# The first expert slot interleaved with the drain of a fused decoder layer, and the order at the slots' ends

## What is computed

```
x = layernorm(x + retention(x))                 # decay mask, group norm over heads and time
x = layernorm(x + cross_attention(x, ctx))      # 16 heads of 16, causal softmax
x = layernorm(x + moe(x))                       # 8 experts, 2 of 8 per token

logits = xf @ router_w.T;  probs = softmax(logits);  topk_probs, topk_idx = top_k(probs, 2)
topk_probs = topk_probs / sum(topk_probs)
h   = gelu_tanh(xf @ w_fc[e] + b_fc[e])         # 256 -> 1024
out = h @ w_proj[e] + b_proj[e]                 # 1024 -> 256, weighted and summed over the 2 experts
```

## Time and profile before

| | |
|---|---|
| median of 3 runs | 1047.76 us (1046.54 to 1048.6) |
| the profiled execution | 1047.56 us, span 1045.7 us |
| TensorE busy | 966.0 us (92%), 11474 matmuls |
| VectorE, ScalarE, GpSimd busy | 640.7 (61%), 585.7 (56%), 371.9 us (36%) |
| sequences, from 0 to | 529 us |
| drain, then slot 0 | 529 to 559 us, 559 to 578 us |
| slots 1 to 35 | 578 to 1012 us |
| output norms | 1012 to 1046 us |

### The profile page before, as it was taken

One profiled execution on the slowest core, in us unless ns is written; L12 is line 12 of the kernel. 1 busy time (PEld: TensorE's weight loads), 2 busy tenths in 40 slices (PEclk: granted clock), 3 DMA queues, 4 the chain that ended last, 5 costly groups with the idle time before them and its releaser, 6 DMA issues.

```text
span 1045.7 us, 31053 instructions
## 1 busy us (share of the span) xinstructions
PE 966.0 (92%) x11474; PEld 875.3 (84%) x11474; DVE 640.7 (61%) x1952; ACT 585.7 (56%) x1531; POOL 371.9 (36%) x630
## 2 busy tenths in 40 slices
PE   6799999999999999999988998999999999999960
PEld 4688888888888888888866998999999999999960
DVE  2466767767667677777754575565564665564436
ACT  3355555555555565655544565565665675566534
POOL 0224444544445444444443422222322222223323
PEclk9899999999999999999979999999999999999985
DMA  7101151111111111111211425422525432522327
GB/s 265 55 22 53 42 175 55 40 62 42 53 62 37 58 43 52 48 47 55 85 42 37 78 41 132 128 44 42 140 42 136 103 73 42 133 48 41 50 35 317
DMA packets 56931, 79.93 MB, mean 76 GB/s; under 512 B 5680, under 2 KB 45872, under 8 KB 56560
## 3 DMA queue, kind: packets, MB, share of 16 engines
q1 hardware_dynamic: 41072, 58.50, 17.5%
q0 software_dynamic: 13536, 18.16, 10.3%
q10 hardware_dynamic: 2208, 1.73, 0.6%
HBM read 52.10 MB, written 29.71 MB: 78 GB/s over the span
## 4 chain that ended last, share of the span: by engine, by line
PE 67%; DVE 15%; issue 5%; ACT 5%; POOL 4%; DMA 3%; SPq 1%; ACTq 0%; DVEq 0%; POOLq 0%
PE bank L703 16%; PE bank L716 16%; DVE row_max L1045 7%; PE bank L468 5%; PE bank L583 3%; PE bank L483 3%; PE bank L458 3%; PE bank L536 3%; PE bank L628 3%; PE bank L508 3%; ACT h_f L967 2%; PE bank L614 2%; PE bank L503 2%; POOL grstd L1384 2%; DVE x_pre L1076 1%
## 5 line engine op out<-in xcount | busy, mean ns | idle before, releaser
L961 ACT ACTIVATE h_hi<-bank,bfc_s 128x256 fp32r<-128x256 f32 x288 | 139.6, 485 | 173.1 <-PE bank L703 171.0
L1247 DVE TENSOR_TENSOR h_lo<-h_f,h_hi 128x256 fp32r<-128x256 f32 x288 | 122.6, 426 | 175.6 <-ACT h_f L967 173.2
L1426 POOL DMA_INDIRECT residual_sum<-y_w,meta_i x72 | 116.6, 1620 | 319.0 <-DVE y_w L1271 299.1
L703 PE MATMUL bank<-xs_hi,w_hi 128*128 128x256 f32 x576 | 167.4, 291 | 8.1 <-DVE xs_lo L1217 7.8
L716 PE MATMUL bank<-w_hi,h_hi 128*128 128x256 f32 x576 | 163.5, 284 | 1.3 <-DVE h_lo L1247 1.3
L716 PE MATMUL bank<-w_hi,h_lo 128*128 128x256 f32 x576 | 163.3, 283 | 0.0
L703 PE MATMUL bank<-xs_lo,w_hi 128*128 128x256 f32 x576 | 163.2, 283 | 0.0
L703 PE MATMUL bank<-xs_hi,w_lo 128*128 128x256 f32 x576 | 162.8, 283 | 0.0
L716 PE MATMUL bank<-w_lo,h_hi 128*128 128x256 f32 x576 | 162.7, 282 | 0.0
L967 ACT ACTIVATE h_f<-bank,bfc_s 128x256 f32<-128x256 f32 x288 | 139.2, 483 | 0.7 <-DVE h_lo L1247 0.7
L703 PEld LDWEIGHTS bank<-xs_hi,w_hi 128*128 128x128 f32 x576 | 109.8, 191 | 9.7 <-issue 9.7
(11 more groups left out here) (167 smaller groups left out, 1977.3 us busy)
## 6 DMA issues: line engine op xcount, KB each, us to landing
rows<-sent_rows SPq DMA_DIRECT2D x37, 258.0 KB
...
```

The costliest lines, as they stand in the source:

```text
L703: last = mm(ps_h[j % 4][:, 0:SLOT], w[:, at:at + P], v[:, k, :], start=(n == 0), stop=(n == 3 * NCH - 1))
L961: A(h_hi[j % 4][:, :], ps_h[j % 4][:, 0:SLOT], ACT.Gelu_apprx_tanh, bias=bias)
L1247: V.tensor_tensor(h_lo[j % 4][:, :], h_f[j % 2][:, :], h_hi[j % 4][:, :].bitcast(f32), ALU.subtract).then_inc(s["h_split"], 1)
L1426: G.indirect_dma_start(total, bass.IndirectOffsetOnAxis(meta_i[:, half:half + 1], 0), y_w[:, half, :], None, compute_op=ALU.add)\
```

## The change

1. **Slot 0 inside the drain.** Its fc and proj stand one by one between the stages of sequences 29 to 31 (`fc0`, `proj0` on PE, `hidden` on ACT, `hidden_low` on DVE), and the 21 idle matmuls are gone. Its hidden columns lie in half of `ps_prep` instead of four banks, so fc j waits for the Gelus of fc j-1. The rows of slot 1 are turned into `ps_y`. `rank_out`, `copies_last`, `last_norms` stand beside slot 1 now, `rank_last`, `last_places` beside slot 2, `count_next` beside slot 3.
2. **The last norm ahead.** In step 31 the maxima of sequence 30 and what follows move from the step to the drain; `ln1_sum` and `ln1_norm` of sequence 31 stand before three of the four maxima, `x1_turn` and the turn of slot 0's rows before `max_turn`. On POOL `shares` of that step stands behind the norm's power.
3. **Low half of the next rows ahead of weights.** `split_rows(g + 1)` moves in front of `last_hi` and the last `split_lo` in a slot.
4. SPLIT is B - 12: the first expert's weights are split one step earlier. On POOL `add(0)` stands before the last sequence's second power, and `add(1)` before its `shares` and `send`.

```diff
-SPLIT = B - 11
+SPLIT = B - 12
...
-        ps_h = bank[0:4]
-        ps_xs = ps_prep
+        def ps_h(g, j):
+
+            if isinstance(g, int) and g == 0:
+                return ps_prep[:, 0:SLOT]
+            return bank[j % 4][:, 0:SLOT]
+
+        def ps_xs(g):
+
+            return ps_y if isinstance(g, int) and g == 1 else ps_prep
...
             def fc(g, j, whi, wlo):
 
-                if j >= 4:
+                if isinstance(g, int) and g == 0:
+                    if j >= 1:
+                        pe.wait_ge(s["h_done"], j + EVER)
+                elif j >= 4:
                     pe.wait_ge(s["h_done"], HC * g + j - 3 + EVER)
                 else:
                     pe.wait_ge(s["h_done"], HC * g + EVER)
+                if isinstance(g, int) and g == 1 and j < NT:
+                    pe.wait_ge(s["att_exp"], 4 * (B - 1) + j + 1)
...
             def rank_out(j):
 
-                if j == 0:
-                    logits(At(B - 2))
                 if j == 1:
                     o_turn(At(B - 1))
                 if j == 3:
                     att_back(At(B - 1))
                 if j == 4:
                     att_proj(At(B - 1))
+                if j == 6:
                     rank(At(B - 2))
                 if j == 8:
                     x2_turn(At(B - 1))
@@ -752,42 +773,55 @@
 
             def drain():
 
-                idle(DRAIN_IDLE)
+                x1_turn(At(B - 1))
+                pe.wait_ge(s["v_out"], B)
+                pe.sem_inc(s["rows_turned"], EVER)
+                turn_rows(0)
+                max_turn(At(B - 2))
+                o_turn(At(B - 3))
+                qx(At(B - 1))
                 att_back(At(B - 3))
-                x1_turn(At(B - 1))
-                idle(DRAIN_IDLE)
                 att_proj(At(B - 3))
-                qx(At(B - 1))
+                fc0(0)
                 att_scores(At(B - 2))
                 rank(At(B - 4))
                 x2_turn(At(B - 3))
                 max_scores(At(B - 1))
                 logits(At(B - 3))
-                pe.sem_inc(s["rows_turned"], EVER)
-                turn_rows(0)
                 att_values(At(B - 2))
+                fc0(1)
                 max_turn(At(B - 1))
                 pe.wait_ge(s["qx_out"], B)
-                idle(DRAIN_IDLE, to=bank_g)
+                proj0(0)
+                fc0(2)
                 o_turn(At(B - 2))
-                idle(DRAIN_IDLE, to=bank_g)
+                proj0(1)
+                fc0(3)
                 att_back(At(B - 2))
-                idle(DRAIN_IDLE, to=bank_g)
+                proj0(2)
+                fc0(4)
+                att_scores(At(B - 1))
                 att_proj(At(B - 2))
-                att_scores(At(B - 1))
+                proj0(3)
+                fc0(5)
                 rank(At(B - 3))
-                idle(DRAIN_IDLE, to=bank_g)
+                proj0(4)
+                fc0(6)
                 x2_turn(At(B - 2))
-                idle(DRAIN_IDLE, to=bank_g)
+                proj0(5)
+                fc0(7)
+                logits(At(B - 2))
+                pe.wait_ge(s["max_split"], B)
+                turn_rows(1)
+                proj0(6)
+                proj0(7)
+                pe.wait_ge(s["xs_ready"], 2)
                 att_values(At(B - 1))
 
             steps(step, between)
-            pe.wait_ge(s["v_out"], B)
             drain()
-            pe.wait_ge(s["w_ready"], HC)
-            pe.wait_ge(s["att_exp"], 4 * B)
-            slot(0, 0, rank_out)
-            slot(1, 0, rank_last)
+            slot(1, 0, rank_out)
+            slot(2, 0, rank_last)
...
             def drain():
 
+                x1_T_out(At(B - 1))
+                xs_high(0)
+                max_hi_out(At(B - 2))
+                max_out(At(B - 2))
+                qx_out(At(B - 1))
                 att_back_out(At(B - 3))
-                x1_T_out(At(B - 1))
-                qx_out(At(B - 1))
+                x2_again(At(B - 4))
                 for r in range(NT):
                     att_exp(At(B - 2), r)
                 x2_T_out(At(B - 3))
+                act.wait_ge(s["consts_expert"], 16 * CONSTS_EXPERT)
+                act.sem_inc(s["h_done"], EVER)
+                hidden(0, 0, 0)
                 o_out(At(B - 2))
-                xs_high(0)
+                hidden(0, 0, 1)
                 max_hi_out(At(B - 1))
+                hidden(0, 0, 2)
                 max_out(At(B - 1))
+                hidden(0, 0, 3)
+                att_back_out(At(B - 2))
+                hidden(0, 0, 4)
                 x2_again(At(B - 3))
-                att_back_out(At(B - 2))
+                hidden(0, 0, 5)
+                hidden(0, 0, 6)
+                x2_T_out(At(B - 2))
+                hidden(0, 0, 7)
+                xs_high(1)
                 for r in range(NT):
                     att_exp(At(B - 1), r)
-                x2_T_out(At(B - 2))
+                x2_again(At(B - 2))
                 o_out(At(B - 1))
-                x2_again(At(B - 2))
 
             act.wait_ge(s["got_small"], 16)
             steps(step, between)
             drain()
-            act.wait_ge(s["consts_expert"], 16 * CONSTS_EXPERT)
-            act.sem_inc(s["h_done"], EVER)
-            slot(0, 0, None, copies_last)
-            for g in range(1, EARLY - 1):
+            slot(1, 0, None, copies_last)
...
+            def hidden_low(g, j):
+
+                dve.wait_ge(s["h_done"], HC * g + j + 1 + EVER)
+                if j >= 4:
+                    dve.wait_ge(s["y_done"], HC * g + j - 3)
+                V.tensor_tensor(h_lo[j % 4][:, :], h_f[j % 2][:, :], h_hi[j % 4][:, :].bitcast(f32),
+                                ALU.subtract).then_inc(s["h_split"], 1)
+
             def slot(g, e, split_to=None, beside=None):
                 for j in range(HC):
-                    dve.wait_ge(s["h_done"], HC * g + j + 1 + EVER)
-                    if j >= 4:
-                        dve.wait_ge(s["y_done"], HC * g + j - 3)
-                    V.tensor_tensor(h_lo[j % 4][:, :], h_f[j % 2][:, :], h_hi[j % 4][:, :].bitcast(f32),
-                                    ALU.subtract).then_inc(s["h_split"], 1)
+                    hidden_low(g, j)
+                    if j == HC - 1:
+                        split_rows(g + 1)
                     if split_to and j == HC - 1:
                         last_hi(*split_to)
                     if split_to:
                         split_lo(*split_to, j)
                     if beside:
                         beside(j)
-                split_rows(g + 1)
+                add_rows(g, e)
...
             def last_norms(j):
 
-                if j == 0:
-                    lg_out(At(B - 2))
                 if j == 1:
                     att_norm(At(B - 1))
-                if j == 2:
-                    pick(At(B - 2))
                 if j == 4:
                     ln2_stats(At(B - 1))
-                    put(At(B - 2))
                 if j == 5:
                     ln2_norm(At(B - 1))
+                if j == 6:
+                    put(At(B - 2))
 
             def last_places(j):
 
@@ -1297,31 +1354,52 @@
 
             def drain():
 
+                ln1_sum(At(B - 1))
+                att_max(At(B - 2), 0)
+                ln1_norm(At(B - 1))
+                for r in range(1, NT):
+                    att_max(At(B - 2), r)
+                max_twice(At(B - 2))
+                lg_out(At(B - 4))
+                for name in ("meta_ready", "h_split", "y_biased"):
+                    dve.sem_inc(s[name], EVER)
+                take_rows(0)
+                split_rows(0)
+                max_split(At(B - 2))
+                att_norm(At(B - 3))
+                pick(At(B - 4))
                 ln2_stats(At(B - 3))
-                pick(At(B - 4))
+                put(At(B - 4))
                 ln2_norm(At(B - 3))
-                put(At(B - 4))
                 for r in range(NT):
                     att_max(At(B - 1), r)
                 max_twice(At(B - 1))
                 lg_out(At(B - 3))
+                hidden_low(0, 0)
                 max_split(At(B - 1))
+                hidden_low(0, 1)
                 att_norm(At(B - 2))
-                for name in ("meta_ready", "h_split", "y_biased"):
-                    dve.sem_inc(s[name], EVER)
-                take_rows(0)
-                split_rows(0)
                 pick(At(B - 3))
+                hidden_low(0, 2)
+                hidden_low(0, 3)
                 ln2_stats(At(B - 2))
+                hidden_low(0, 4)
+                ln2_norm(At(B - 2))
+                hidden_low(0, 5)
                 put(At(B - 3))
-                ln2_norm(At(B - 2))
+                hidden_low(0, 6)
+                lg_out(At(B - 2))
+                hidden_low(0, 7)
+                split_rows(1)
+                pick(At(B - 2))
+                add_rows(0, 0)
 
             steps(step)
+            dve.wait_ge(s["consts_expert"], 16 * CONSTS_EXPERT)
             drain()
```

(12 more changed lines are left out.)

80 lines of the change are left out of this document (49 added, 31 removed).

## The result

The changed kernel took 1041.91 us (median of 7 executions, 1038.86 to 1044.5), the kernel before 1046.54 beside it (7, 1043.89 to 1048.6): a ratio of 0.9955 with an interval of 0.9937 to 0.9972, which is 4.7 us (the medians differ by 4.6). In a second set of executions the ratio was 0.9944 [0.9927, 0.9961]. The forecast was 10.6 us. The time lies just inside the range (its upper end was 1042.0), but the gain is less than half of what the sum gave. In the comparisons of this document executions that ran at about half clock throughout, or were disturbed otherwise, are left out.

What follows compares the result with a forecast made beforehand. Bound by TensorE: after the drain everything is in series on it, with gaps in the drain, slot 0 and the first expert's slots. 6.4 - 0.3 + 4.5 = 10.6 us off 1047.6 gives 1037.0; range 1033.5 to 1042.0.

Steps and rivals of the forecast that it cites:

- A: Drain with slot 0: interleaving gains 8.4 us at full clock, less 2.0 for half clock: 6.4 us.
- B: Fetch of the first expert's rows, needed in mid slot 3: loss between 0 and 3.4 us, taken as -0.3.
- the walk: PE, ACT and DVE stepped through the new drain with profiled durations: slot 3 starts at 594.05 against 602.42, 8.4 us gained.
- rival 1: Drain, 541 to 565 us: the clock does not come back, all at half; slower, 1049.6 us; 4%.
- This edit alone gives nothing: Drain: the last norm ahead gains 0, as `att_scores` still waits for the maxima; it only makes room.
- rival 4: SyncE's fetch of slot 4's rows is late, the 3.4 us gap moves into slot 3: 1040.2 us; 8%.
- C: Order in the expert slots: `xs_lo` first ends most of PE's 7.8 us of waits; 4.5 us gained, bounds 2 and 6.1.
- grown to about 5: Sign of being right: PE's one wait for the next rows, in expert 0, grows from 3.2 to about 5 us.
- 2: Drain on ACT: a change of table costs more than its load, 2.6 us more on the chain: 1039.6; 12%.
- 3: Drain: the clock stays full from 541 us on, 2.0 us more gained: 1034.5 to 1035; 14%.
- 5: Expert slots' new order gives nothing: 1041.5, 3%; or the drain hardly gains, engines waiting in turn: 1, 1042.4, 6%.
- slot 1 from 565 to 568: Sign of being right: after the drain, slot 1 starts at 565 to 568 us, following the second Gelu load.

Runs made afterwards that it cites:

- experiment 8: Changed kernel with next rows fetched ahead of the weights and 29 idle matmuls: 1032.02 us; with 19 of them and exponentials early: 1030.35 and 1031.38 us.

## Where the prediction was wrong, and where right

**A, the drain, was the wrong step**: 6.4 forecast, 2.55 in the means of the profiles, and with B 6.1 forecast and 2.6 timed. The sum stood on one profile of before and one walk, and the miss can be taken apart in three. *The walk:* slot 3 started 5.3 us earlier in the profile (603.40 to 598.06), 1.1 less than forecast. The rounds of the hidden columns came a little later (559.5 for 558.4; I had taken the signals at their least), and slot 1's first hidden column and the end of the exponentials were later again. *The reference:* the profile of before had 13.6 us of half clock in its drain. It is one of two kinds that the old drain shows; the mean of six profiles is 1.06 shorter, and that much less was there to be gained. *The rest:* I had taken 4 us at half clock for the new drain, and the first profile had 3.4; five more had 10.2 to 13.6, and their mean with it is 1.64 later. 6.4 - 1.1 - 1.06 - 1.64 = 2.6.

How much of that is the clock and how much the walk can be read from the two profiles with 29 idle matmuls, which have no half clock at all in the drain: both took 77.36 to slot 3. The walk at full clock gives 84.04 - 8.4 = 75.6. If the idle matmuls themselves cost nothing there (in experiment 8 they may have), the walk was short by 1.7, and half clock cost the six new drains 80.43 - 77.36 = 3.1 on average, for the 2.0 in the sum. So **the walk, which has the engines wait for each other too little, is the largest part of the miss (1.7), before the clock (1.1) and the reference (1.06)**. That split is an estimate, but the first profile bears it out: its clock was full up to 565.2, and the exponentials were over at 565.45, by then already 1.35 late. There was far more half clock than I had assumed, 11.3 us on average in the new drain and not 4, but a microsecond of it cost less (0.27, not 0.5). The old drain, with its 21 idle matmuls, had 10.2 on average. So the new drain does not keep the clock: rival 1's mechanism, at a small part of its price.

Idle matmuls in these places bring the clock back: no half clock in the drain in three profiles. The profile with the early exponentials had none either, but the slower executions of that kernel, at a lower mean clock, speak against this being so every time. What it is worth in time is shown only by 1 to 2 us of medians.

"This edit alone gives nothing" of the first norm was half of a truth. Undone beside the rest of the change it cost some 3 us, with more half clock than in any other drain. The walk had looked at the chain of `att_scores` only.

**B was right in the first profile and half of what it is on average**: slot 3 took 12.07 for 11.83, 0.24 for the 0.3, but the mean of the six profiles is 0.62. In three later profiles it took 13.0 to 13.3, with waits for the rows of 0.5 to 0.7, so rival 4 happens, at 1 us.

**C was right in kind and too large by 1.1** in the profile (3.39 for 4.5, slot 4 to slot 35), by 1.6 in the ratio of the order alone. In six experts the first slot gained 1.2 to 1.6 and the one behind it lost 0.4 to 0.8: together 0.78 to 0.86, forecast 0.85. In expert 0 slots 4 and 5 lost 1.29 and not 0.75. The fetch left 16.1 us after slot 4's start, not 15.3 (so 0.8 later, where I had 0.75), but needed 8.2 us (625.22 to 633.4), not 7.6. That wait "grown to about 5" was 5.4. Slot 27 is 0.29 longer in every profile of the new drain and in none of the old, with or without the order, so this loss is not C's; its cause is open. What I did not see is what the one fetch behind the weights held back: put first, it gave 7 us on top of the change (1041.91 to 1035.05), more than the change itself, and with it the order gives 6.2 on the old drain.

**The rivals.** 1 did not happen (no stretch of 12 us of work at half clock from 541 to 565 in a profile, nor a slower kernel). 2 is refuted by the row of the load. 3, full clock from 541 on, held up to 565 in one profile and is not the rule. 4 comes and goes at 1 us. 5 has two halves: that the order gives nothing is refuted; that the drain hardly gains, because the engines wait for each other in turn (A is 1), is not, since 2.55 lies nearer to 1 than to 6.4. It had 6%. Against what I wrote for the profile: slot 1 from 565 to 568 came (567.5), slot 3 from 594 to 597 was just missed (597.1), the waits for `xs_lo` are 0.

**The chances.** Faster, with 0.93, was right. All cases shared one reference, the drain of one profile, and none of them was "the profile of before is itself slower there than the usual execution". That the time fell inside the range owes something to the reference too: the forecast was taken off 1047.6, and the kernel before took 1046.54 beside the changed one, about 1 us of the miss hidden.

## What to carry to other kernels

Where the granted clock moves, a single profile is not a baseline: measure the stage from its own start mark in several profiles, and write how much of it was at half clock. When work is moved into gaps, count what is left idle at the new gaps too; gaps filled with matmuls that compute nothing cost little here and took away most of the spread. And before an order is tuned so that an engine comes earlier, look at what the queue behind it has in front: here 2 MB of weights ahead of 256 KB of rows held back half of what the new order in the slots gives on the old drain, and one transfer placed first gave more on top of the change than the change had.

## What the runs showed of the chip

The same kernel spreads over 3 to 8 us from execution to execution in one set, and within a set the time goes roughly with the mean granted clock: before, 1041.8 us at 0.978, 1046.4 at 0.973, 1049.7 at 0.968; the changed kernel 1038.9 at 0.975 and 1044.5 at 0.968. The clock is not all of it: in the last set the kernel before took 1048.2 and 1048.7 at 0.975, and the loop's last work on VectorE started anywhere from 519.3 to 521.7 us. The half-clock stretches moved between executions of one kernel (the first profile of before had them from 531.3 and 541.6, the second from 534.6 and 561.9). A change of the activation table cost 1.29 us on a busy ScalarE in both directions.
